# A recommendation model on one core: the first and last chunk of the cross network made half as wide, the first computed in plain fp32

## What is computed

```python
item_img = gelu(LN(emb @ mm_w + mm_b));  target = item_table[item_id] + item_img
seq = item_table[item_seq]                                 # 2048 x 50 x 128, rows gathered from HBM
x = concat([t, seq, t - seq, t * seq]);  scores = relu(x @ aw1 + ab1) @ aw2 + ab2
hist = softmax(mask(scores)) @ seq                          # attention pooling
sparse = stack([like, view, item_id, item_img, hist])       # 5 fields of 128
se = sparse * gates(sparse)                                 # small gate network
dnn_in = concat([se, 10 products (se_i @ bil_W[i]) * se_j]) # 15 features of 128 = 1920
xc = dnn_in
for i in range(2): xc = dnn_in * (xc @ cross_K[i] + cross_bias[i]) + xc   # 1920 x 1920 each
h = gelu(LN(xc @ w1 + b1)); h = gelu(LN(h @ w2 + b2)); out = sigmoid(h @ w3 + b3)
```

## Time and profile before

| | |
|---|---|
| median of 3 runs | 2115.8 us (2112.77 to 2117.34) |
| profiled execution | 2113.03 us, its span in the trace 2111.2 us |
| PE busy | 1928.6 us (91%) |
| DVE / ACT / POOL busy | 1337.5 / 914.2 / 894.6 us |
| mean granted PE clock | 0.946 |
| DMA moved | 220.31 MB, mean 104 GB/s |

### The profile page before, as it was taken

One profiled execution on the slowest core, in us unless ns is written; L12 is line 12 of the kernel. 1 busy time (PEld: TensorE's weight loads), 2 busy tenths in 40 slices (PEclk: granted clock), 3 DMA queues, 4 the chain that ended last, 5 costly groups with the idle time before them and its releaser, 6 DMA issues. The chain is left out here.

```text
span 2111.2 us, 32903 instructions
## 1 busy us (share of the span) xinstructions
PE 1928.6 (91%) x9608; PEld 1513.0 (72%) x9608; DVE 1337.5 (63%) x2248; ACT 914.2 (43%) x1987; POOL 894.6 (42%) x854
## 2 busy tenths in 40 slices
PE   1666558999999999999999999999999999999997
PEld 1444336777777887777777886777777888888886
DVE  4555564767777755667777755667777654445553
ACT  1433343454544335654444235654445233322234
POOL 7777776556556511555556501555560000000000
PEclk6766669999999999999999999999999999999998
DMA  5112113334434452334434452334332353333320
GB/s 165 50 48 53 50 50 102 104 100 132 117 110 120 144 192 69 99 90 124 125 105 125 142 184 69 99 94 127 118 109 92 111 175 126 89 99 96 98 68 1
DMA packets 99679, 220.31 MB, mean 104 GB/s; under 512 B 21792, under 2 KB 27184, under 8 KB 99376
## 3 DMA queue, kind: packets, MB, share of 16 engines
q1 hardware_dynamic: 63072, 136.90, 21.3%
q0 software_dynamic: 27136, 55.63, 10.5%
q10 hardware_dynamic: 9296, 25.70, 3.3%
HBM read 205.29 MB, written 12.85 MB: 103 GB/s over the span
## 5 line engine op out<-in xcount | busy, mean ns | idle before, releaser
L440 POOL DMA_INDIRECT e<-in_item_table,idx_all x800 | 843.7, 1055 | 650.9 <-issue 302.1
L1212 DVE TENSOR_TENSOR Wl<-raw,Wh 128x640 fp32r<-128x640 f32 (+1 forms) x411 | 331.9, 807 | 267.0 <-DVEq L1211 265.8
L855 ACT ACTIVATE Wh<-raw 128x640 fp32r<-128x640 f32 (+1 forms) x411 | 296.0, 724 | 470.6 <-ACTq L854 467.6
L575 PE MATMUL xps<-X0h,Wh 128*128 128x512 f32 x900 | 364.1, 404 | 1.4 <-PEq L573 1.4
L575 PE MATMUL xps<-X1h,Wh 128*128 128x512 f32 x900 | 359.4, 399 | 0.0
L577 PE MATMUL xps<-X0h,Wl 128*128 128x512 f32 x900 | 351.6, 391 | 0.0
L576 PE MATMUL xps<-X0l,Wh 128*128 128x512 f32 x900 | 351.2, 390 | 0.0
L577 PE MATMUL xps<-X1h,Wl 128*128 128x512 f32 x900 | 351.0, 390 | 0.0
L576 PE MATMUL xps<-X1l,Wh 128*128 128x512 f32 x900 | 350.7, 390 | 0.0
L814 ACT ACTIVATE e<-e,pw 128x128 f32<-128x128 f32 x800 | 242.9, 388 | 15.5 <-ACTq L139 15.5
L577 PEld LDWEIGHTS xps<-X0h,Wl 128*128 128x128 f32 x900 | 169.1, 188 | 37.0
(11 more groups left out here) (159 smaller groups left out, 2196.7 us busy)
## 6 DMA issues: line engine op xcount, KB each, us to landing
raw<-in_cross_K SPq DMA_DIRECT2D x360, 320.0 KB
raw<-in_w SPq DMA_DIRECT2D x51, 256.0 KB
e<-in_item_table,idx_all POOLq DMA_INDIRECT x800, 2.5
dnn_scratch<-dn ACTq DMA_DIRECT2D x12, 960.0 KB
x1f<-dnn_scratch ACTq DMA_DIRECT2D x3, 2048.0 KB, 9.6
x1f<-dnn_scratch ACTq DMA_DIRECT2D x3, 1792.0 KB, 15.2
e<-in_w SPq DMA_DIRECT2D x9, 256.0 KB, 4.6
dn<-in_embT SPq DMA_DIRECT2D x1, 1024.0 KB, 5.3
```

The costliest lines, as they stand in the source:

```text
L440: nc.gpsimd.indirect_dma_start(out=dst, out_offset=None, in_=table, in_offset=bass.IndirectOffsetOnAxis(ap=idx_all[:, t, s:s + 1], axis=0) ...
L575: m0 = mm(out, wh, Xh[:, 0:T, k, :], start=(k == 0), stop=False)
L855: af(Wh[:, split_slot(w), 0:n], raw[:, rs, 0:n], ACT.Copy).then_inc(hi_done, 1)
L1212: v.tensor_tensor(Wl[:, rs, 0:n], raw[:, rs, 0:n], Wh[:, slot, 0:n].bitcast(F32), ALU.subtract).then_inc(lo_done, 1)
```

## The change

The chunks become 2, 4, 4, 4 and 2 tiles. The opening handles 2 tiles, chunk 0 has 2 tiles and carries the attention of 4, chunk 3 that of 2 (every other step), chunk 4 none. Chunk 0 is computed with plain fp32 matmuls from the blocks as they are loaded and from `x0f`, `x1f` in fp32: no splits of weights or activations in this chunk. Each such matmul is one row in the listing of instructions and two in the trace. `AHEAD` goes from 5 to 6.

```diff
-TILES = (4, 4, 4, 4)
+TILES = (2, 4, 4, 4, 2)
-AHEAD = TILES[0] + 1
+AHEAD = TILES[0] + TILES[1]
...
+            def first_products(layer, n, kg):
+                x, T = (x0f, x1f)[layer], TILES[0]
+                out = by_tile(xps[:, n % BANKS, :], 0)
...
+                pe.wait_ge(raw_landed[rs], DMA).then_inc(raw_landed[rs], -DMA)
+                for i in range(KG):
+                    k = kg * KG + i
...
+                    last = mm(out, raw[:, rs, i * P:(i + 1) * P], x[:, 0:T, k, :], start=(k == 0), stop=(k == FEATS - 1))
+                    if i == 0 and w:
+                        last.then_inc(w_free, 1)
...
+            def first_w1():
...
+                    for b in range(T):
...
+                        last = mm(xps[:, b, :], x0f[:, b, k, :], raw[:, rs, 0:H1], start=(k == 0), stop=(k == FEATS - 1))
...
             def products(c, layer, n, kg):
+                if c == 0:
+                    first_products(layer, n, kg)
+                    return
...
-                if c * STREAM + b + LOOK < ENDING:
+                if STREAM <= c * STREAM + b + LOOK < ENDING:
                     w_hi(c * STREAM + b + LOOK)
...
+            def first_scale(layer, n):
+                T = TILES[0]
+                dve.wait_ge(mm_done, 1).then_inc(mm_done, -1)
+                v.scalar_tensor_tensor(out=(x1f, x0f)[layer][:, 0:T, n, :], in0=by_tile(xps[:, n % BANKS, :], 0),
+                                       scalar=col("cb", layer * FEATS + n), in1=x0f[:, 0:T, n, :], op0=ALU.add, op1=ALU.mult).then_inc(scaled, 1)
...
+            def first_end(layer, n):
...
+                if layer == 1:
+                    done(v.tensor_tensor(x0f[:, 0:T, n, :], x0f[:, 0:T, n, :], x1f[:, 0:T, n, :], ALU.add))
+                dve.sem_inc(x_ready, 1)
```

More of the change, by code:

```diff
@@ L550, in tail_turn, with tail_bilinear @@
                 last.then_inc(tp_ready, 1)
-            def tail_bilinear():
+            def tail_bilinear(t):
                 pe.wait_ge(seT_ready, 1).then_inc(seT_ready, -1)
                 pe.wait_ge(bank4_free, 1).then_inc(bank4_free, -1)
+                x = x0f[:, t] if t < TILES[0] else dn
                 for i in range(4):
-                    last = mm(mps[:, i * P:(i + 1) * P], bil[:, i, :], dn[:, i, :], start=True, stop=True)
+                    last = mm(mps[:, i * P:(i + 1) * P], bil[:, i, :], x[:, i, :], start=True, stop=True)
@@ L557, in tail_bilinear @@
                 last.then_inc(m_ready, 1)
+            def first_products(layer, n, kg):
+                x, T = (x0f, x1f)[layer], TILES[0]
+                out = by_tile(xps[:, n % BANKS, :], 0)
+                if kg == 0:
+                    pe.wait_ge(bank_free, 1).then_inc(bank_free, -1)
+                w = (layer * FEATS + n) * UNITS + kg
+                rs = raw_slot(w)
+                pe.wait_ge(raw_landed[rs], DMA).then_inc(raw_landed[rs], -DMA)
+                for i in range(KG):
+                    k = kg * KG + i
+                    if n == 0:
+                        pe.wait_ge(x_ready, 1).then_inc(x_ready, -1)
+                    last = mm(out, raw[:, rs, i * P:(i + 1) * P], x[:, 0:T, k, :], start=(k == 0), stop=(k == FEATS - 1))
+                    if i == 0 and w:
+                        last.then_inc(w_free, 1)
+                if kg == UNITS - 1:
+                    last.then_inc(mm_done, 1)
@@ new lines, in first_w1 @@
+            def first_w1():
+                T = TILES[0]
+                assert 1 < T < BANKS
+                for k in range(FEATS):
+                    w = BLOCKS + k
+                    rs = raw_slot(w)
+                    pe.wait_ge(raw_landed[rs], DMA).then_inc(raw_landed[rs], -DMA)
+                    pe.wait_ge(x_ready, 1).then_inc(x_ready, -1)
+                    for b in range(T):
+                        if k == 0:
+                            pe.wait_ge(bank_free, 1).then_inc(bank_free, -1)
+                        last = mm(xps[:, b, :], x0f[:, b, k, :], raw[:, rs, 0:H1], start=(k == 0), stop=(k == FEATS - 1))
+                        if b == 0:
+                            last.then_inc(w_free, 1)
+                        if b == 1 and k < FEATS - 1:
+                            last.then_inc(x0_free, 1)
+                last.then_inc(mm_done, 2)
+                for b in range(T, BANKS):
+                    pe.wait_ge(bank_free, 1).then_inc(bank_free, -1)
@@ L607, in w1_products @@
             def w1_products(c):
+                if c == 0:
+                    first_w1()
+                    return
                 T = TILES[c]
@@ L970, in step @@
                     weigh(*p.summed)
-                if p.n or p.layer:
+                if c and (p.n or p.layer):
                     x_hi(*((c, p.layer, p.n - 1) if p.n else (c, 0, FEATS - 1)))
@@ L997, in w1_stage @@
                     unit(c, BLOCKS + k)
-                    if k == 0:
+                    if c and k == 0:
                         x_hi(c, 1, FEATS - 1)
@@ L1016, in _ @@
                 opening_step(p)
-                if p.k == 6:
-                    for w in range(LOOK):
-                        w_hi(w)
             for c in range(CHUNKS):
@@ L1179, in tail_gate_apply, with tail_pairs @@
                 dve.sem_inc(se_ready, 1)
-            def tail_pairs():
+            def tail_pairs(t):
+                x = x0f[:, t] if t < TILES[0] else dn
                 dve.wait_ge(m_ready, 1).then_inc(m_ready, -1)
+                if t == LAST:
+                    dve.sem_inc(x_ready, FIELDS)
                 at = FIELDS
@@ L1191, in tail_pairs @@
                 dve.sem_inc(bank4_free, 1)
[L1192 to L1199, removed]
-                    dve.sem_inc(x_ready, FEATS - FIELDS)
[L1201 to L1206, removed]
+                if t >= TILES[0]:
+                    dve.sem_inc(dn_full, 1)
+                elif t == LAST:
+                    dve.sem_inc(x_ready, FEATS - FIELDS)
             def w_lo(w):
@@ L1237, in x_scale @@
             def x_scale(c, layer, n):
+                if c == 0:
+                    first_scale(layer, n)
+                    return
                 dve.wait_ge(sum_done, 1).then_inc(sum_done, -1)
@@ L1243, in x_end @@
             def x_end(c, layer, n):
+                if c == 0:
+                    first_end(layer, n)
+                    return
                 T, xn = TILES[c], fresh(c, layer, n)
@@ L1444, in _ @@
                 opening_step(p)
[L1445 to L1448, removed]
             for c in range(CHUNKS):
```

47 lines of the change are left out of this document (20 added, 27 removed).

## The result

| | before | after |
|---|---|---|
| median | 2116.3 us (2112.77 to 2117.34, 4 runs) | 2131.2 us (2130.3 to 2132.5, 4 runs) |
| profiled execution, its span | 2113.03, 2111.2 | 2132.02, 2129.9 |
| PE busy | 1928.6 us | 1962.5 us |
| DMA moved | 220.31 MB | 257.82 MB |

The ratio is 1.0064, 95% interval 1.0052 to 1.0076: slower by 0.6%, on the side that was forecast, and 9 us above the forecast time of 2122.

The account below looks back on a forecast made before the run. After an opening that waits for gathers, TensorE bounds the kernel, with splits deciding chunk 4. First product 183, chunk 1 at 519, chunk 4's cross layers 1874 to 2074, tail 43 plus 2: span 2119, time 2122 us; range 2111 to 2136.

Parts of the forecast that it names:

- The opening: Start of the kernel: two tiles of gathers fewer take 136.8 us away, first product at 183 instead of 324.
- Chunk 0: Its cross layers: fp32 passes 193.5 us plus attention 107, gathers at the same pace, 6 added for waits: end at 490.
- Chunk 0's w1: w1 stage of chunk 0: 25.6 us of fp32 matmuls plus 3 for loads, so chunk 1 starts at 519.
- Chunks 1 to 3: Middle chunks: chunk 1 ends at 984, chunk 2 at 1457, chunk 3 at 1874.
- The loop: Layer 1 of chunk 4: chain around DVE and ACT takes 6.5 us a step against PE's 5.4; layer 97.5 us.
- the term for layer 0: Layer 0 of chunk 4: 82 us plus some 18 for the fc of four tiles with its waits, 100 together.
- the lead: Chunk 4's cross layers: three blocks of lead give back some 4 us once.
- Burst and change of layer: Chunk 4: nine last w1 blocks loaded in one go ahead of block 12, and the layer change, cost 6 us.
- The tail: End of the kernel: w1 8.2, final products and fc 12.6, 22 behind the last product: 43, plus 2 for late splits.
- The last chunk was not PE's: Rival, chunk 4: gaps between short operations close more, the chunk takes 175 us, time 2097; chance 0.20.
- The lost clock: Rival, chunk 0: some 14 gather waits each halve the clock, 22 us, 15 on the path, time 2137; chance 0.15.
- The weight loads: Rival, chunk 4: a 256-column matmul takes as long as its load's row, 0.188 us, time 2185; chance 0.05.

Follow-up runs that it names:

- Experiment 7: The changed kernel with AHEAD = TILES[0] + 1 = 3, so gathers of chunk 0's last tiles come by fives: 2186.5 us, ratio 1.0328 to the kernel before.
- Experiment 1: The changed kernel, with ACT in the last chunk splitting w_hi of block 3k+4 ahead of x_hi: 2110.0 us, ratio 0.9963 to the kernel before.
- Experiment 3: Experiment 1 with the fc's LN statistics of tiles 2 and 3 made in step 1 instead of step 0 of the last chunk: 2109.6 us, ratio 0.9966.

## Why the forecast came out as it did

The direction and its cause were as forecast; by stages (starts in us, predicted against measured):

| | predicted | measured |
|---|---|---|
| first product | 183 | 182.5 |
| last gather of tile 5 | 430.7 | 430.8 |
| end of chunk 0's cross layers | 490 | 488.9 |
| chunk 1 | 519 | 519.1 |
| chunk 2 | 984 | 979.2 |
| chunk 3 | 1457 | 1454.9 |
| chunk 4 | 1874 | 1874.8 |
| end of chunk 4's cross layers | 2074 | 2082.2 |
| end | 2119 | 2129.9 |

**The opening** came out, in part by luck: tile 1's last gather starts at 142.5 where I had 145.2, and from it to the first product it is 40.0 us where I had 38. So did the last gather of tile 5: tile 2's first starts at 147.5 instead of 152.3, and from there to tile 5's last it is 283.4 us instead of 278.4. The two errors cancel. **Chunk 0**: passes of 0.215 us and the pace of the gathers gave 484, I added 6 for waits and measured 5 over it; PE has eight waits there, 7.0 us in all, the longest 1.4. Experiment 7 shows that the gathers' pace is a bound there, and by how much tens move it.

**Chunk 0's w1** took 30.2 where I had 28.6 (120 passes of 0.215 are 25.8, not 25.6). Windows in the stage: the mean busy share of the DMA engines and GB/s are the last two numbers.

```profile
493.00:500.00 7.00, 6.45 (x16) 2.55 (x14) 0.00 (x0) 0.00 (x0) 1.95 (x3) 1.00 1.00 387
500.00:506.00 6.00, 5.62 (x12) 1.96 (x12) 3.70 (x6) 4.27 (x8) 3.73 (x4) 1.00 1.03 398
```

My bound of 333 GB/s, scaled from a stage at a share of 0.63, was too low: at a share of 1.0 they moved 387 to 398. PE waits all the same, three times 0.3 to 0.7 us and 1.44 us for the first product of chunk 1. That the former are waits for loads which full DMA engines hold up is argued from the windows; no run took the transfers away.

**Chunks 1 to 3** are within 5 us each, and within 1 together: 4.9 too long for chunk 1, 2.7 and 2.9 too short for the others.

**The loop** of layer 1 was forecast at 6.5 us and measured at 6.50, with waits of 0.88 for `w_ready`; the layer at 97.5 and 96.0. Experiment 1 took one link out, and 15 us went from this layer. That the link was there only because of the order on ACT I did not see: the prediction took the order as given, which it was.

**What failed is the term for layer 0.** I had 82 + 18, less 4 for the lead; 111.3 were measured. In rows: PE's own 81 + 12.2 make 93.2; 13.0 us of waits (6.5 for `w_ready`, 6.1 at the fc's transposes, 0.4); and 5.1 more. Of these some 3.3 are an estimate for a clock at half, which the sum did not have: 32 products 0.213 us apart instead of 0.12, and four transposes in 0.73 us instead of 0.39. The rest lies in the starts right behind the waits. The waits begin in the first steps of the chunk, where DVE does the statistics of four tiles in one piece (L1313 and L1314) before the next `w_lo`, and PE waits 2.9 us. From the timelines of DVE and PE:

```profile
1882.53 0.69 DVE L1313 BATCH_NORM_STATS2 tiny<-dn 128x6 f32<-128x512 f32 x1 [0.24 <-DVEq L1239]
...
1887.64 0.82 DVE L1229 TENSOR_TENSOR Wl<-raw,Wh 128x640 fp32r<-128x640 f32 x1
...
1888.75 0.36 PE L616 MATMUL xps<-X0h,Wh 128*128 128x256 f32 x1 [2.89 <-PEq L610]
...
1889.68 0.41 PE L617 MATMUL xps<-X0l,Wh 128*128 128x256 f32 x1
1889.89 0.42 PE L618 MATMUL xps<-X0h,Wl 128*128 128x256 f32 x1
...
1893.94 1.09 PE L692 MATMUL xps<-ident,dn 128*128 128x128 f32 x4 [2.35 <-PEq L690]
```

The products at 1889.68 and 1889.89 start 0.21 us apart instead of 0.12; the granted clock is at half, 1.2 of 2.4 GHz, from 1889.6 for 10.2 us, and in that stretch PE waits again (2.35 us, last row). Experiment 3 shows that moving half of these statistics moves the wait only.

**Burst and change of layer**, 6 in the sum: the burst did not show. ACT waits in the last chunk for free split slots and for `x_end`, never for a block to land. The change of layer is one wait of 1.9 us. So layer 0 was 15 us too small in the sum, this term and layer 1 together some 7 too large: the 8 us by which chunk 4 came out over the forecast are what was left of 15 after errors the other way.

**The tail** took 47.7 for 45. The w1 products took 12.4 us for 8.2; in experiment 1, where the splits run further ahead, 10.3.

**The rivals.** The last chunk was not PE's. Two swapped lines make its layer 1 PE's, and the time is then 2110.0; it stays above the 2097 of this rival, since layer 0 keeps 10 us of waits and a dip of the clock (0.97 in its window). The lost clock did not come in chunk 0: waits stayed at 1.4 us and less, and the granted clock at 0.99 and 1.00, as the argument against it had it. With gathers by fives it did come, at 0.93. The Trainium skill ("TensorE: Matmul & The Clock Gate", section "HAM oscillation — how this bites in real kernels") describes short bursts behind DMA waits that start cold: that fits experiment 7, with waits for gathers of up to 9.7 us, and the start of chunk 4, with a wait for splits of 2.9. The prediction said that by the page's rule this rival would hold. That goes further than the page: the kernel it describes waits about 3 to 5 us ahead of each burst, and the waits expected here were of 1 to 2. The weight loads did not show: 0.12 us from start to start.

**Chances.** The forecast had 0.50, and 2131 lies in its own range of 2111 to 2136.

**Slips in the prediction.** It reads the slices of the page as 9 from the seventh on and 5 to 6 before; the seventh is an 8 and the first a 1. By its own terms the rival of the weight loads comes to 2189 (2122 - 200 + 254 + 13), not 2185. Neither bears on the forecast.

## What to carry to other kernels

When a tile dimension is halved, list what is not halved with it; here the weight splits and the fixed order of two engines around each other, which a step of 10.2 us had hidden and one of 5.4 did not. Then look for the link of that loop which is there only by program order: swapping two lines on ACT was worth 21 us in the small chunk and nothing in the large one, and it turned a loss of 0.6% into a gain of 0.4%. Work that lies in the shadow of another bound, as the attention in an opening that waits for gathers, is not free when that shadow is shortened: 54 of the 141 us went back this way.

## What was not expected of the hardware

- On two tiles plain fp32 from the loaded blocks beats three fp32r products with their splits by 63 us in this kernel, although PE itself has more to do (299.5 against 291.0 us busy in the cross layers, the latter at a granted clock of 0.93). DVE has 97 us less to do there and PE waits less for ACT; that this is the whole gain is argued, and the split kernel had the old order on ACT.
- Eight waits, none over 1.4 us, left the granted clock at 0.99 and 1.00 in chunk 0. Behind one of 2.9 us in chunk 4 it was at half for 10.2 us.
- With the DMA engines at a share of 1.0, weight blocks, features and gathers together moved 387 to 398 GB/s.
